# Second and third edge pass of a graph network: the window blocks take turns in two PSUM banks, and ScalarE takes a block out after all six index copies

## The reference, cut to what matters

```
x_src = x[src]
agg = segment_sum(x_src, dst * R + etype, n * R)
cnt = segment_sum(ones, dst * R + etype, n * R)
out = einsum('nrd,rdk->nk', agg / max(cnt, 1), W) + x @ root + bias
```

## Time and profile before

| | us |
|---|---|
| three runs | 5401.39, 5415.35, 5419.33 |
| median | 5415.35 |
| the profiled execution | 5398.16 |
| its span, first to last instruction | 5396.4 |
| mean granted TensorE clock | 0.794 of full speed |
| PE busy | 3765.6 (70%) |
| DVE busy | 2663.4 (49%) |
| POOL busy | 2356.5 (44%) |
| ACT busy | 1163.5 (22%) |

### The profile page before, as it was taken

One profiled execution on the slowest core, in us unless ns is written; L12 is line 12 of the kernel. 1 busy time (PEld: TensorE's weight loads), 2 busy tenths in 40 slices (PEclk: granted clock), 3 DMA queues, 4 the chain that ended last, 5 costly groups with the idle time before them and its releaser, 6 DMA issues.

```text
span 5396.4 us, 103191 instructions
## 1 busy us (share of the span) xinstructions
PE 3765.6 (70%) x20688; PEld 3046.7 (56%) x20691; DVE 2663.4 (49%) x6964; ACT 1163.5 (22%) x3868; POOL 2356.5 (44%) x2346
## 2 busy tenths in 40 slices
PE   4777677788888766666666776767676766757873
PEld 1333566666666655555555555656565655656762
DVE  7654454444444455545544544444444444892235
ACT  0122111121222111111222222222222222441112
POOL 0000465555555454545555555556555553003430
PEclk8999788888889877766766667887777776888886
DMA  2022333444444322222222223333333432436640
GB/s 73 32 66 75 103 108 114 117 120 118 119 126 133 110 55 55 55 58 64 76 76 74 77 82 104 109 109 108 104 105 107 111 107 67 170 134 176 179 118 12
DMA packets 478385, 526.90 MB, mean 98 GB/s; under 512 B 96596, under 2 KB 398238, under 8 KB 474670
## 3 DMA queue, kind: packets, MB, share of 16 engines
q1 hardware_dynamic: 252780, 246.52, 14.7%
q0 software_dynamic: 85824, 199.51, 13.8%
q10 hardware_dynamic: 139746, 80.46, 5.1%
HBM read 399.82 MB, written 126.39 MB: 98 GB/s over the span
## 4 chain that ended last, share of the span: by engine, by line
PE 31%; issue 25%; DMA 9%; DVE 9%; another core or an unknown queue 7%; POOL 6%; ACTq 4%; ACT 3%; DVEq 3%; SPq 2%; POOLq 1%
DMA msg_r<-y_tab,idx_r 7%; PE psum L1616 6%; POOL msg_r L635 6%; PE psum L1894 3%; PE psum L1689 2%; PE psum L1618 2%; PE psum L1804 1%; DVE shot_r L1151 1%; PE psum L1765 1%; PE psum L1805 1%; DVE h_t L1413 1%; ACT idx_r L712 1%; PE psum L1554 1%; PE psum L1542 1%
## 5 line engine op out<-in xcount | busy, mean ns | idle before, releaser
L635 POOL DMA_INDIRECT msg_r<-y_tab,idx_r x2160 | 2198.1, 1018 | 2327.9 <-issue 1115.5
L1616 PE MATMUL psum<-shot_r 128*128 128x200 f32 x2604 | 982.1, 478 | 404.8 <-issue 207.7
L1145 DVE SCALAR_TENSOR_TENSOR shot_r<-edge_f,win_base,iota 128x600 bf16<-128x600 f32 x434 | 366.3, 844 | 1437.3 <-remote 849.4
L712 ACT COPY idx_r<-row_i 128x1 int32 x2142 | 396.0, 191 | 1921.3 <-DMA msg_r<-y_tab,idx_r 1092.7
L1616 PEld LDWEIGHTS psum<-shot_r 128*128 128x128 f32 x2604 | 542.0, 258 | 438.4 <-issue 433.6
L1689 PE MATMUL psum<-hot_r,msg_r 128*128 128x128 f32 x2880 | 510.4, 320 | 162.1 <-DMA msg_r<-y_tab,idx_r 134.9
L1804 PE MATMUL psum<-msg_r,shot_r 128*128 128x128 f32 x1440 | 394.1, 364 | 305.4 <-DMA msg_r<-in_attr 103.7
L1689 PEld LDWEIGHTS psum<-hot_r,msg_r 128*128 128x128 f32 x2880 | 420.8, 219 | 231.4 <-DMA msg_r<-y_tab,idx_r 143.7
L1131 DVE TENSOR_SCALAR hot_r<-iota,edge_g 128x128 f32<-128x128 f32 x1602 | 446.4, 354 | 181.4 <-PE psum L1805 90.3
L1618 PEld LDWEIGHTS psum<-shot_r 128*100 128x100 bf16 x2604 | 430.2, 165 | 128.6 <-issue 20.3
L1804 PEld LDWEIGHTS psum<-msg_r,shot_r 128*128 128x128 f32 x1440 | 279.1, 241 | 375.2 <-issue 183.2
(11 more groups left out here) (315 smaller groups left out, 4746.5 us busy)
## 6 DMA issues: line engine op xcount, KB each, us to landing
msg_r<-in_attr SPq DMA_DIRECT2D x882, 64.0 KB
h_t<-count_tab SPq DMA_DIRECT2D x25, 1600.0 KB, 6.7
w_tab<-shot_r ACTq DMA_DIRECT2D x385, 100.0 KB
count_tab<-shot_r ACTq DMA_DIRECT2D x385, 100.0 KB
h_t<-w_tab SPq DMA_DIRECT2D x24, 1600.0 KB
msg_r<-y_tab,idx_r POOLq DMA_INDIRECT x2160
xn<-heavy_tab SPq DMA_DIRECT2D x76, 320.0 KB
y_tab<-y_s SPq DMA_DIRECT2D x25, 640.0 KB, 2.9
```

The source lines that it names most:

```text
L635: pool.indirect_dma_start(out=msg_r[:, q, 0:width], out_offset=None, in_=table, in_offset=bass.IndirectOffsetOnAxis(ap=idx_r[:, q:q + 1], ...
L712: nc.scalar.copy(idx_r[:, q:q + 1], of[:, q:q + COLS - U + 1][:, bass.ds(c0, 1)]).then_inc(s_idx[k], 1)
L1145: V.scalar_tensor_tensor(out=key_b, in0=of(KEY, KW), scalar=win_base[:, bass.ds(w, 1)], in1=to(KW), op0=ALU.subtract, op1=ALU.is_equal).th ...
L1616: T.matmul(win_ps, low_f[:, i, :], weighted_f[:, i, :], start=False, stop=False)
```

## The change

A function `block_sums(k, blocks)` now gives the place of a block's sums. In pass 0 it is bank 2 as before. In passes 1 and 2 it is bank 2 for a block of even number and bank 4 for one of odd number, from a register. TensorE then waits before a block of number n for one take-out fewer, so that block n - 1 may still be in its bank. ScalarE takes the block out behind all six index copies of the group, in passes 1 and 2. Before pass 1 TensorE waits once for the last block of pass 0 to be out.

```
+        def block_sums(k, blocks):
+            at = slice(2, 3) if k == 0 else bass.ds(blocks.eng.snap(blocks.number() % 2 * 2 + 2), 1)
+            return (psum[:, at, 0:KW].rearrange("p o n -> p (o n)"),
+                    psum[0:TURN, at, 2 * P:4 * P].rearrange("p o (b n) -> p (o b) n", b=2),
+                    psum[:, at, SPARE:SPARE + 1].rearrange("p o n -> p (o n)"))
...
-            def window_out_of_psum():
+            def window_out_of_psum(k):
                 n, w = act_blocks.number(), act_blocks.window()
+                win_ps, count_ps, _ = block_sums(k, act_blocks)
...
-                    if q == UH:
-                        window_out_of_psum()
+                    if k == 0 and q == UH:
+                        window_out_of_psum(k)
                     if chunk is not None:
                         next_row(k, of, c0, before16, q)
+                if k > 0:
+                    window_out_of_psum(k)
...
-            def window_sums():
+            def window_sums(k):
                 v0, v1 = pe_blocks.visits()
+                win_ps, count_ps, spare = block_sums(k, pe_blocks)
                 alone(pe)
-                pe.wait_ge(s_wgone, pe_blocks.number() + 1)
-                clear(psum[:, 2, SPARE:SPARE + 1])
+                pe.wait_ge(s_wgone, pe_blocks.number() + 1 if k == 0 else pe_blocks.number())
+                clear(spare)
...
-                close(psum[:, 2, SPARE:SPARE + 1], s_wsum)
+                close(spare, s_wsum)
...
             pe.wait_ge(s_y_ev[0], TILES + 1)
+            alone(pe)
+            pe.wait_ge(s_wgone, n_rest + 1)
             T.matmul(heavy_next, b2_s[0:1, :], ones[0:1, :], start=False, stop=False)
```

More of the change, by code:

```diff
@@ L376, in share @@
             return eng.snap(n * (D - 1) // WIDE + 1, min_val=1, max_val=MOST)
-        win_ps, count_ps = psum[:, 2, 0:KW], psum[0:TURN, 2, 2 * P:4 * P].rearrange("p (b n) -> p b n", b=2)
+        def block_sums(k, blocks):
[3 more added lines that the diff above has]
+                    psum[:, at, SPARE:SPARE + 1].rearrange("p o n -> p (o n)"))
         w_in = [h1_t[:, slot, :].rearrange("p (w n) -> p w n", w=WPT) for slot in range(2)]
@@ L825, in extra1 @@
             def extra1(D, last):
-                window_out_of_psum()
+                window_out_of_psum(1)
             def hidden2(D):
@@ L853, in _ @@
             with act.Fori(0, more) as i:
-                window_out_of_psum()
+                window_out_of_psum(2)
                 n = act_blocks.number()
@@ L1625, in group_sums @@
                 if k < 3:
-                    window_sums()
+                    window_sums(k)
                 for q in range(U):
@@ L1786, in extra1 @@
             def extra1(D, last):
-                window_sums()
+                window_sums(1)
                 pe_blocks.fetch()
@@ L1826, in _ @@
             with pe.Fori(0, more) as i:
-                window_sums()
+                window_sums(2)
                 pe_blocks.fetch()
```

## The result

The changed kernel takes 5475.82 us (median of 7 runs, 5466.06 to 5490.11), the kernel before 5412.73 us (7 runs, 5369.62 to 5443.70) on the same chip: ratio 1.0132, 95% interval 1.0103 to 1.0162. It is slower by 1.3%: the ratio's excess is 71 us, and the medians lie 63 us apart. The forecast was 5424 us, no change that can be told from noise.

What follows compares the result with a forecast made beforehand. Waits, not a full engine, were taken to bound passes 1 and 2, in a loop of PE, VectorE and POOL. Terms 0 + 0 + 0 + 2 + 8.6 = 10.6 us gave 5426 on the median's level; forecast 5424 us, range 5350 to 5472.

Steps and rivals of the forecast that it cites:

- PE's wait for the take-out: PE's clearing in pass 1: the 35.0 us wait goes, but the first matmul still waits for hot columns; gain 0.
- The bank was no brake: Denies a rival: PE's 25 waits for the take-out are real stops, so its sums start earlier; 5380 us, chance 0.13.
- The second bank doesn't hasten `s_seen`: PE's block-end event to VectorE, passes 1 and 2: a second bank should leave its timing alone; no gain counted.
- a sign of being wrong: POOL's stops for PE, forecast to stay near 431 and 251 us; shrinking by over 30 us would refute the forecast.
- The index copies: ScalarE's three late copies come earlier, POOL's fourth gather has 2.6 us slack: gain 0; as rival brake 5367 us, chance 0.14.
- The register steps: Extra ISA rows on PE and ScalarE, mainly ahead of a visit's first matmul: 8.6 us added, bounds 0 and 45.
- The take-out later on ScalarE: Take-out between a group's last index copy and the next group's first work: 2 us in all, upper end 95 us.
- The slower rival: Register steps in every visit's see-to-matmul path and ScalarE's late ones in 112 groups: 5471 us; chance 0.30, half-size included.

Runs made afterwards that it cites:

- a_banks: Against the kernel before: two alternating banks and PE's shorter wait alone, take-out in the middle of a group in all passes; ratio 1.0041, +22 us.
- c_not_at_end: Changed kernel, but take-out in the middle of the last group of each pass-2 tile; ratio 1.0048 against the kernel before, +26 us.
- p_after: The changed kernel run again, on a chip where the kernel before took 4914.41 us; ratio 1.0031 against it, +15 us.
- d_at_end: Against the kernel before: two banks, take-out late only in the last group of each pass-2 tile, elsewhere in the middle; ratio 1.0178, +95 us.
- group 4: Follow-up runs on one chip, kernel before 4914.41 us: changed kernel +15 us, bank register always 2 -4, deferred tile-end work -2, earlier attribute loads -84.
- group 1: Four kernels parting the change on one chip, kernel before 5331.92 us: +22 and +26 us without late take-out at tile ends, +63 and +95 with it.
- groups 1, 3 and 5: Follow-up runs, each group on its own chip beside the kernel before, which took 5331.92, 5335.34 and 5416.58 us; the changed kernel rerun in the second lost 80 us.
- groups 2 and 4: Follow-up runs, each group on its own chip beside the kernel before, which took 4919.32 and 4914.41 us; the changed kernel rerun in the second lost 15 us.
- q_steps: Kernel before with the bank's number computed into a register but always 2, on a chip where before took 5416.58 us; ratio 1.0011, +6 us.
- m_steps: Kernel before with the bank's number computed into a register but always 2, on a chip where before took 4914.41 us; ratio 0.9992, -4 us.
- e_steps: Kernel before with the bank's number computed into a register but always 2, on a chip where before took 4919.32 us; ratio 1.0001, 0 us.

## Why the prediction was wrong

*PE's wait for the take-out: right in the main.* In pass 1 the 35.0 us in 25 times are gone; the same waits of the changed kernel, for the clearing (L1489) and the block's first matmul (L1626), are

```profile
PE psum L1626 <- DVE shot_r L1160: 210.1, 94, 9.8
...
PE psum L1626 <- issue: 99.2, 67, 3.3
...
PE psum L1489 <- issue: 5.6, 17, 0.5
```

From first to last gather the kernel before has 185.9 us in 85 times for VectorE and 105.1 us in 49 times under "issue". So 24 of the 35 us went over to other waits at the same place, and 11 did not; pass 1 is 13 us shorter in this profile. In a_banks all of it went over: 212.8, 108.8 and 9.6 us, together 331, for 326 before. The bank was no brake: a_banks, in which the wait is gone as well, is 22 us slower. The Trainium skill's advice to rotate groups of matmuls through banks (Perfetto Trace Analysis, section Optimizing Tensor Performance (Matmuls)) holds for what it speaks of, the evacuation's wait; here that wait was not the last.

*The second bank doesn't hasten `s_seen`: right in pass 2.* VectorE's waits with a late update ("remote") are 443.2 us before and 461.5 after; in pass 1 they are 173.2 and 144.5. The prediction named as a sign of being wrong that POOL's stops for PE shrink by more than 30 us: in pass 1 they went from 441.9 us to 376.2, but those for index copies rose from 28.8 to 68.5, and in pass 2 they grew by 79.

*The index copies: right on the chips of this kind.* c_not_at_end, which has them early in all but 24 groups of pass 2, gains nothing on a_banks. On the other kind they may be what makes the groups inside the tiles shorter (p_after above); no run shows it by itself.

*The register steps: small, as forecast.* 8.6 us forecast, 0, -4 and +6 measured, with intervals of 10 us or more to either side. The working has a slip: two steps at 0.103 us are 0.21 us, not the 0.15 in its upper bound, which would be 62 us and not 45. And the sum gives 5426 us on the median's level; why the forecast says 5424 isn't said.

*The take-out later on ScalarE: this step failed.* It said: "I cost it at 2 us in all." What stands queued behind the take-out was listed, as plain ones in pass 2 and, "at the tile ends of pass 1", the table rows and counts. The timeline read for it was the inside of a group of pass 2, where the take-out ends 1.5 us before the ones can start. `hidden2`, which pass 2 has at its own tile ends, isn't in the list. There the take-out's 3.1 us come ahead of some 3 us of other work that was already the last thing before the ones, and only the 0.9 us in which ScalarE waited for PE's sums lie under it. For the 2 us forecast the runs showed 60 us more in pass 2 of the profile (51 in the first groups of the tiles) and 73 us between a_banks and d_at_end. Its own upper end, 95 us, was worked out for the wrong place (112 groups at 0.85 us) and then dropped, since ScalarE is busy 27% of the pass; a share of busy time says nothing of 23 moments in which it is the one waited for.

Even with the place found, the size would have been hard to tell. The take-out less the 0.9 us of cover is 2.2 us, 23 times 51 us, if all is on the path; in group 4 PE's idle time grew by 24 us for it and the pass not at all. On chips like the one of the result the row is pushed later into the next gathers, and its steps take 1.4 us longer each time (last section), another 32 us of row.

*The slower rival* had the number, 5471 us for a measured 5476, by luck, and not the mechanism: register steps and late ones in every group. Its steps measured 6 us at most, and its late ones sit at 23 tile ends.

## What to carry to other kernels

When an operation moves to the end of a loop body, read what the engine does behind the last turn of the loop, in each loop that shares the body, and not only the timeline of a middle turn. Work in an in-order queue costs by what is queued behind it: on the chip of group 1 the same late take-out was harmless in 216 groups and cost some 3 us in each of the other 24. If the row at a boundary is the path, move something out of that row: here that took the whole loss away with the change left in.

## What the hardware showed that was not expected

The kernel before took 5332 to 5417 us in four of the six comparisons (the result's and groups 1, 3 and 5) and 4919 and 4914 us in groups 2 and 4, and the traces of the two kinds differ in two things. I call them kinds of chip; each group had a chip of its own and was run once, so something else that differed between the groups isn't excluded.

First, single steps of ScalarE's, VectorE's and SyncE's own queues take 0.70 us in place of 0.03 to 0.06. The changed kernel's tile loop on ScalarE (L772: count, ns min/median/max, first and last start in us):

```profile
L772 ACTq FUSED_REGOPS  x66: 5/59/727, 685.1 to 4553.1; - x66
L772 ACTq ALU_OP  x66: 6/35/727, 780.3 to 4585.3; - x66
L772 ACTq COMPARE_BRANCH  x66: 5/50/720, 780.4 to 4585.3; - x66
```

and the same kernel in group 4 (p_after):

```profile
L772 ACTq FUSED_REGOPS  x66: 59/59/65, 664.2 to 4067.8; - x66
L772 ACTq ALU_OP  x66: 35/35/35, 744.8 to 4097.0; - x66
L772 ACTq COMPARE_BRANCH  x66: 34/50/54, 744.8 to 4097.0; - x66
```

Counted over the four queues (PE's, ScalarE's, VectorE's, SyncE's) from pass 0's first gather to pass 2's last, transfers left out, steps of 0.66 to 0.76 us number 786 before and 819 after, 660 to 812 in the other kernels of groups 1, 3 and 5, and 16 to 38 in groups 2 and 4. On ScalarE in the changed kernel 226 steps of 11258 are such; 196 of them lie 3 to 8 us after a row of six gathers began, and 3 in its first 3 us, though as many steps lie there. This fits that the steps from `hidden2` to the ones, pushed 2 us later into the gathers, take 4.8 us in place of 3.4.

Second, PE's semaphore updates come late. VectorE's waits for PE over the whole kernel before:

```profile
DVE shot_r L1145 <- remote: 849.4, 162, 13.0
```

There is no such row in the kernels of groups 2 and 4. Bursts of four or more of PE's updates less than 0.12 us apart number 217 in the three passes before, 205 in q_steps, and none in m_steps. In pass 2 before there are 93, each behind the sixth gather of a row, and 80 of them begin 2.0 to 2.6 us after its start (median 2.3). The earlier trace rows show one: the take-out starts 5 us after the block was closed. On such chips a median group of pass 2 takes 9.7 to 9.9 us (before, groups 1 and 3), on the others 8.8 to 8.9 (e_steps, m_steps, p_after). That the gathers hold the updates back and slow the steps is what their times suggest; the run made to test it met the other kind of chip, so it isn't shown, nor is why the kinds differ.
